# A two-layer graph attention kernel: h recomputed from x1 instead of stored, x1 written late, two steps of an epilogue moved to ACT

## What is computed

```python
h = relu(layernorm(x))
wh = h @ W;  e = wh @ a[:128] + (wh @ a[128:]).T
e = where(e > 0, e, 0.2 * e);  e = where(adj > 0, e, -9e15)
x1 = x + elu(softmax(e) @ wh)
h = relu(layernorm(x1))
Qn, Kn = cos_normalize(h @ Wq.T), cos_normalize(h @ Wk.T)
att = softmax(where(adj > 0, Kn @ Qn.T, -9e15))
out = x1 + 0.5 * (att @ h) + 0.5 * h
```

## Time and profile before

| | us |
|---|---|
| median of 3 runs | 2189.89 |
| lowest and highest | 2189.19, 2190.89 |
| profiled execution | 2189.39 |
| its span | 2187.6 |
| busy: PE, DVE, ACT, POOL | 2142.1, 1963.5, 1752.8, 33.0 |

### The profile page before, as it was taken

How to read it: one execution, slowest core, us unless ns; L and a number is a source line. 1 busy time by engine, 2 the same in 40 slices (tenths; PEclk the granted TensorE clock), 3 DMA queues, 4 the chain that set the end, 5 groups by cost and what they waited for, 6 DMA issues and landing times.

```text
span 2187.6 us, 63203 instructions
## 1 busy us (share of the span) xinstructions
PE 2142.1 (98%) x26185; PEld 1733.5 (79%) x26185; DVE 1963.5 (90%) x1686; ACT 1752.8 (80%) x1928; POOL 33.0 (2%) x43
## 2 busy tenths in 40 slices
PE   5999999999999979999999999999999999999998
PEld 5999999999999956777777777777777777777776
DVE  7999999999999858889888898898898898898987
ACT  6687778878788668888888888888888888888886
POOL 1000000000000030000000000000000000000000
PEclk9999999999999989999999999999999999999999
DMA  6899999999999916565565665665665666656653
GB/s 248 328 382 401 390 405 397 401 402 399 403 400 388 361 40 217 193 223 204 207 215 196 224 212 196 220 220 193 214 221 200 212 204 216 215 194 218 218 193 115
DMA packets 153732, 573.52 MB, mean 262 GB/s; under 512 B 9936, under 2 KB 10576, under 8 KB 153168
## 3 DMA queue, kind: packets, MB, share of 16 engines
q1 hardware_dynamic: 142176, 546.02, 68.3%
q10 hardware_dynamic: 11376, 24.91, 3.0%
HBM read 558.24 MB, written 12.65 MB: 261 GB/s over the span
## 4 chain that ended last, share of the span: by engine, by line
PE 95%; DVE 2%; ACT 1%; issue 1%; DMA 0%; POOL 0%; ACTq 0%; POOLq 0%; DVEq 0%
PE bank L1197 32%; PE bank L1245 30%; PE bank L1266 21%; PE bank L1261 10%; DVE hl_buf L726 1%; PE bank L1152 1%; PE bank L1172 0%; DVE hl_buf L714 0%; DMA ring<-adj 0%; ACT hl_buf L558 0%; ACT ring L619 0%; POOL hl_buf L401 0%; PE bank L1094 0%; PE bank L1134 0%; DMA q_buf<-x 0%
## 5 line engine op out<-in xcount | busy, mean ns | idle before, releaser
L619 ACT ACTIVATE ring<-bank,th_col 128x512 f32<-128x512 f32 x1024 | 647.1, 683 | 231.0 <-PE bank L1245 223.3
L988 DVE SCALAR_TENSOR_TENSOR ring<-ring 128x2048 f32<-128x2048 int32 x256 | 586.4, 2291 | 154.5 <-ACT ring L619 154.5
L1197 PE MATMUL bank<-v_buf,ring 128*128 128x129 f16 (+1 forms) x12288 | 711.9, 220 | 6.3 <-DVE ring L902 6.1
L1197 PEld LDWEIGHTS bank<-v_buf,ring 128*128 128x128 f16 x12288 | 707.8, 98 | 9.8 <-issue 8.9
L1245 PE MATMUL bank<-v_buf,q_buf 128*128 128x512 f16 x3072 | 706.4, 380 | 5.2 <-ACT ring L619 5.2
L1266 PE MATMUL bank<-u_buf,hl_buf 128*128 (+1 forms) x8192 | 704.3, 220 | 0.0
L1266 PEld LDWEIGHTS bank<-u_buf,hl_buf 128*128 128x128 f16 x8192 | 631.8, 98 | 55.9
L902 DVE SCALAR_TENSOR_TENSOR ring<-r_ring,th_word,ring 128x1024 f32<-128x1024 f32 x512 | 619.3, 1277 | 19.3 <-ACT ring L448 19.1
L993 DVE TENSOR_TENSOR hl_buf<-ring,hl_buf 128x2048 f16<-128x2048 f32 x256 | 584.5, 2284 | 0.0
L1261 PE MATMUL bank<-u_buf,hl_buf 128*128 (+1 forms) x2048 | 557.9, 272 | 0.5 <-DVE hl_buf L993 0.5
L448 ACT ACTIVATE ring<-ring 128x2048 f32<-128x2048 int32 x256 | 481.2, 1908 | 88.4 <-DMA ring<-adj 85.0
(11 more groups left out here) (138 smaller groups left out, 433.0 us busy)
## 6 DMA issues: line engine op xcount, KB each, us to landing
ring<-adj SPq DMA_DIRECT2D x512, 1024.0 KB, 5.6
r_ring<-a_rows SPq DMA_DIRECT2D x8, 512.0 KB, 7.0
x_dram<-q_buf ACTq DMA_DIRECT2D x8, 512.0 KB, 7.2
h_dram<-hl_buf ACTq DMA_DIRECT2D x8, 512.0 KB, 7.4
r_ring<-x_dram ACTq DMA_DIRECT2D x16, 256.0 KB, 4.2
r_ring<-h_dram ACTq DMA_DIRECT2D x16, 256.0 KB, 4.4
out<-r_ring ACTq DMA_DIRECT2D x16, 256.0 KB, 4.8
r_ring<-k_rows ACTq DMA_DIRECT2D x15, 256.0 KB, 4.1
```

Source lines behind the costliest of these rows:

```text
L619: ins = nc.scalar.activation(p_ring[:, k, (2 * hf + m) * IW:(2 * hf + m + 1) * IW], bank[:, 2 * hf + m, :], ACT.Exp, scale=q_scale[:, j:j ...
L988: V.scalar_tensor_tensor(p_ring[:, k, :], adj_ring[:, k, :], 0.0, p_ring[:, k, :], ALU.is_gt, ALU.mult).then_inc(s_m, 1)
L1197: ins = mm(acc0(par, it), weights0(k, ps)[:, it // 4, jj, f], v2[:, bass.ds((2 * j + us) * VW, D + 1)], start=False, stop=False, skip_grou ...
```

## The change

- DRAM no longer holds h. For the last sum of layer 1, `residual_h` computes it again from the loaded x1 with four Relus of 128 x 128 on ACT, at step (3, 2) of each chunk (in the first one at (2, 2)); for that, scale and bias of all 64 tiles are kept, each chunk's in its own columns.
- x1 of chunks 0, 4 and 7 is written as before, from ACT. That of 1, 5, 2, 6 and 3 is written from SP directly after the last load of adj for layer 0. Each copy of transposed h waits for the two writes whose memory it overwrites, on one of four semaphores.
- DVE's min(z, 0) goes. ACT computes relu(-z) and then exp(-that) in its place, one behind the other.
- DVE's cast of h to float16 goes. ACT copies h there behind its Relus, where it issued the write of h; DVE waits for that copy and subtracts.

Cut to its core (semaphores' declarations and the renaming of columns in `scale_bias` are left out):

```diff
+X1_EARLY = (0, 4, 7)
+X1_LATE = (1, 5, 2, 6, 3)
...
             chunks0(chunk)
+            for c in X1_LATE:
+                sp.wait_ge(s_ev, len(EPI0) * c + EPI0.index("x1") + 1)
+                sp.dma_start(x1_dram[:, c * C0:(c + 1) * C0], xs[:, c * C0:(c + 1) * C0]).then_inc(s_x1w[c % (NC0 // 2)], 16)
...
                 def exponential():
-                    act.wait_ge(s_ev, at("neg"))
-                    nc.scalar.activation(e_buf, e_buf, ACT.Exp).then_inc(s_ea, 1)
+                    act.wait_ge(s_free, c + 1)
+                    nc.scalar.activation(e_buf, z_buf, ACT.Relu, scale=-1.0).then_inc(s_neg, 1)
+                    act.wait_ge(s_neg, c + 1)
+                    nc.scalar.activation(e_buf, e_buf, ACT.Exp, scale=-1.0).then_inc(s_ea, 1)
 
                 def root():
-                    act.wait_ge(s_ev, at("x1"))
-                    act.dma_start(x1_dram[:, bass.ds(c * C0, C0)], xs[:, bass.ds(c * C0, C0)]).then_inc(s_x1w, 16)
+                    if c in X1_EARLY:
+                        act.wait_ge(s_ev, at("x1"))
+                        act.dma_start(x1_dram[:, bass.ds(c * C0, C0)], xs[:, bass.ds(c * C0, C0)]).then_inc(
+                            s_x1w[c % (NC0 // 2)], 16)
...
                     if lo == 0:
                         act.wait_ge(s_ev, at("nbias"))
-                        if not (isinstance(c, int) and c == 0):
-                            act.wait_ge(s_hw, 16 * c)
...
                     ins.then_inc(s_ea, 1)
                     act.wait_ge(s_ea, 3 * c + 3)
-                    act.dma_start(h_dram[:, bass.ds(c * C0, C0)], h_buf).then_inc(s_hw, 16)
+                    nc.scalar.activation(u_buf[:, bass.ds(c * IT0, IT0), 0:D], h_buf.rearrange("p (t f) -> p t f", f=D),
+                                         ACT.Copy).then_inc(s_uh, 1)
...
-            act.wait_ge(s_x1w, 16 * (NC0 - 1))
-
             def copy_ht(g):
+                act.wait_ge(s_x1w[g // 4], 32)
                 act.wait_ge(s_ht, g + 1)
...
-            act.wait_ge(s_x1w, 16 * NC0)
             copy_ht(12)
...
-            act.wait_ge(s_hw, 16 * NC0)
...
             def residual(i):
                 act.dma_start(e_x1, x1_dram[:, bass.ds(i * IW, IW)]).then_inc(s_fin, 16)
-                act.dma_start(e_h, h_dram[:, bass.ds(i * IW, IW)]).then_inc(s_fin, 16)
+
+            def residual_h(i):
+                act.wait_ge(s_fin, 16 * (i + 1))
+                for it in range(IT1):
+                    f, t = slice(it * P, (it + 1) * P), i * IT1 + it
+                    ins = nc.scalar.activation(e_h[:, f], e_x1[:, f], ACT.Relu, bias=nbias[:, t:t + 1], scale=rstd[:, t:t + 1])
+                ins.then_inc(s_eh, 1)
...
-                def negative():
-                    dve.wait_ge(s_free, c + 1)
-                    V.tensor_scalar(e_buf, z_buf, 0.0, None, ALU.min).then_inc(s_ev, 1)
...
-                    V.tensor_copy(hi, h8).then_inc(s_ev, 1)
-                    dve.wait_ge(s_ev, at("hi"))
+                    dve.wait_ge(s_uh, c + 1)
                     V.tensor_tensor(u_buf[:, bass.ds(c * IT0, IT0), D + 2:UW], h8, hi, ALU.subtract).then_inc(s_ev, 1)
...
-            dve.wait_ge(s_x1w, 16 * (NC0 - 1))
-
             def copy_ht(g):
+                dve.wait_ge(s_x1w[g // 4], 32)
...
-            dve.wait_ge(s_x1w, 16 * NC0)
             copy_ht(13)
...
-                    dve.wait_ge(s_fin, 32 * (i + 1))
+                    dve.wait_ge(s_eh, i + 1)
```

More of the change, by code:

```diff
@@ L59 @@
 EARLY = 4
+X1_EARLY = (0, 4, 7)
+X1_LATE = (1, 5, 2, 6, 3)
 FOLDS = (0, 16, 48, T)
 LN = ("diff", "total", "m2", "dsq", "between", "var", "rstd", "nbias")
-EPI0 = ("den", "neg", "elu", "x1", "stats") + LN + ("hi", "lo")
+EPI0 = ("den", "elu", "x1", "stats") + LN + ("lo",)
 EPI1 = ("some", "max", "recip", "scale", "keep", "kept", "lows", "y")
@@ L77, in graph_layers @@
         x1_dram = nc.dram_tensor("x1_dram", [P, N], F32, kind="Internal").ap()
-        h_dram = nc.dram_tensor("h_dram", [P, N], F32, kind="Internal").ap()
         k_rows = nc.dram_tensor("k_rows", [T, P], F32, kind="Internal").ap()
@@ L185, in graph_layers @@
         s_ev = sem("epilogue0_vector")
+        s_neg = sem("negative_part_ready")
+        s_uh = sem("h_high_ready")
         s_ea = sem("epilogue0_scalar")
-        s_x1w = sem("x1_written")
-        s_hw = sem("h_written")
+        s_x1w = [sem(f"x1_written{p}") for p in range(NC0 // 2)]
+        s_eh = sem("residual_h_ready")
         s_wkq = sem("wkq_in")
@@ L515, in normalised @@
                         ins = nc.scalar.activation(h_buf[:, it * P:(it + 1) * P], xs[:, bass.ds(c * C0 + it * P, P)],
-                                                   ACT.Relu, bias=nbias[:, it:it + 1], scale=rstd[:, it:it + 1])
+                                                   ACT.Relu, bias=nbias[:, c * IT0 + it:c * IT0 + it + 1],
+                                                   scale=rstd[:, c * IT0 + it:c * IT0 + it + 1])
                     if hi < IT0:
@@ L653, in chunk1 @@
                     quotient, store = epilogue1(i - 1, 1 - par)
-                    parts = {(0, 2): lambda: key_high(i + 1), (1, 1): quotient, (2, 1): store, (2, 2): lambda: residual(i),
+                    parts = {(0, 2): lambda: key_high(i + 1), (1, 1): quotient, (2, 1): store, (2, 2): lambda: residual(i), (3, 2): lambda: residual_h(i),
                              (2, 3): lambda: load_factors(i + 2)}
@@ L660, in chunk1 @@
                 else:
-                    parts = {(0, 0): lambda: load_factors(1), (1, 2): lambda: key_high(1), (2, 1): lambda: load_factors(2)}
+                    parts = {(0, 0): lambda: load_factors(1), (1, 2): lambda: key_high(1), (2, 1): lambda: load_factors(2),
+                             (2, 2): lambda: residual_h(0)}
                 for g in range(G1):
@@ L699, in variance, with scale_bias @@
                 V.scalar_tensor_tensor(var, sq, 1.0 / D, var, ALU.mult, ALU.add).then_inc(done, 1)
-            def scale_bias(lo, hi, at, done):
-                V.reciprocal(rstd[:, lo:hi], small[:, 4, lo:hi]).then_inc(done, 1)
+            def scale_bias(lo, hi, at, done, base=0):
+                to = slice(base + lo, base + hi)
+                V.reciprocal(rstd[:, to], small[:, 4, lo:hi]).then_inc(done, 1)
                 dve.wait_ge(done, at("rstd"))
-                V.scalar_tensor_tensor(nbias[:, lo:hi], small[:, 1, lo:hi], -0.5, rstd[:, lo:hi],
+                V.scalar_tensor_tensor(nbias[:, to], small[:, 1, lo:hi], -0.5, rstd[:, to],
                                        ALU.mult, ALU.mult).then_inc(done, 1)
@@ L843, in scales @@
                     dve.wait_ge(s_ea, 3 * c + 2)
-                    scale_bias(0, IT0, at, s_ev)
+                    scale_bias(0, IT0, at, s_ev, c * IT0)
                 def split():
@@ L849, in split @@
                     hi = u_buf[:, bass.ds(c * IT0, IT0), 0:D]
-                    V.tensor_copy(hi, h8).then_inc(s_ev, 1)
-                    dve.wait_ge(s_ev, at("hi"))
+                    dve.wait_ge(s_uh, c + 1)
                     V.tensor_tensor(u_buf[:, bass.ds(c * IT0, IT0), D + 2:UW], h8, hi, ALU.subtract).then_inc(s_ev, 1)
-                return denominators, negative, residual, moments, scales, split
+                return denominators, residual, moments, scales, split
             def split_weights():
@@ L889, in chunk @@
                 else:
-                    parts = dict(zip((3, 7, 10, 11, 15, 19), epilogue(c - 1, 1 - par)))
+                    parts = dict(zip((3, 10, 11, 15, 19), epilogue(c - 1, 1 - par)))
                     if c == 1:
@@ L946, in key_low @@
                                 ALU.subtract).then_inc(s_lo, 1)
-            denominators, negative, residual, moments, scales, split = epilogue(NC0 - 1, 1)
+            denominators, residual, moments, scales, split = epilogue(NC0 - 1, 1)
             copy_ht(1)
@@ L958, in _ @@
             copy_rows(0)
-            negative()
             copy_ht(7)
```

## The result

| us | before | after |
|---|---|---|
| median of 20 runs each | 2190.67 | 2194.72 |
| lowest and highest | 2189.19, 2194.53 | 2192.73, 2199.20 |
| ratio of the times, with its 95% interval | | 1.0019 (1.0013 to 1.0026) |
| profiled execution | 2189.39 | 2196.39 |
| its span | 2187.6 | 2194.5 |

So the change costs 4.05 us, between 2.8 and 5.7. The median lies just under the 0.2% (4.4 us) named ahead, though the interval reaches beyond it; the time is inside the forecast range, 0.3 us under its top, and the cost is four times the +1.05 of the forecast sum. The traces tell where, the medians how much.

The account below looks back on a forecast made before the run. PE was taken to bound the kernel, except between the layers. Terms -0.4 + 0 + 0 + 1.1 + 0.55 - 0.2 + 0 = +1.05 us took 2189.89 to 2190.9; range 2188.2 to 2195, chance 0.80.

Parts of the forecast that it names:

- Traffic in layer 0: Layer 0: removing seven h and five x1 writes gives 0 us, as PE's unit takes the same with idle DMA.
- The rival by which DMA set the pace: Layer 0: DMA bandwidth bounds PE after all, so dropping twelve writes saves 15.8 us, giving 2174; chance 0.05.
- The -0.4 for the last load: End of layer 0: less traffic and a lighter DVE shorten PE's waits for the first copies of transposed h; -0.4 us.
- Late writes: End of layer 0: five x1 writes behind the last load on its own queue cost 0 us, bounds 0 and 2.5.
- the late writes hold the last load: Rival, before PE's first q and k product: the load ends with all writes, 6.6 us more, 2197.5; chance 0.10.
- The Relu in chunks 1 to 6: Layer 0, forecast for chunks 1 to 7: ACT's Relu hides beside PE, 0 us, bounds -0.3 and +0.5.
- The Relu between the layers: Last epilogue: the Exp waits for the Relu on ACT's path, +1.1 us (0.95 to 1.3).
- The cast: Between the layers: ACT's Copy of h delays the key's high part, +0.55 us, bounds 0.5 and 0.75.
- Layer 1's start: Before layer 1's first exp: one DMA issue of h less, -0.2 us, bounds -0.35 and 0.
- Layer 1: Layer 1 chunks: four recomputing Relus, a 1.6 us burst on ACT, fit within 2.5 us of slack; 0 us.
- the table rival: Layer 1: ACT changes tables for Relu beside Exp; PE waits 0.75 us per chunk, 12 us, 2203; chance 0.03.
- The clock: Between the layers, PE's longer idle stretch behind the Exp: one low-clock stretch more or less, 2 us either way; chance 0.02.

Follow-up runs that it names:

- a5: The changed kernel with the late x1 writes waiting for the last load's landing and min(z, 0) back on DVE; median 2190.75 us, ratio to before 1.0002.
- a7: The changed kernel with late writes after the last load's landing, and both the minimum and the cast of h back on DVE; 2191.17 us, ratio 1.0002.
- a1: The changed kernel with SP waiting for the last adjacency load to land before it issues the five late x1 writes; 2193.15 us, ratio 1.0010.
- a10: a7 with the Relus that recompute h at step (3, 0) of each chunk instead of (3, 2); 2190.28 us, ratio to before 0.9994.
- a2: The changed kernel with all eight x1 writes issued by ACT in their epilogues, none late; 2192.43 us, ratio to before 1.0009.
- b2: The kernel before with only the negative part moved: Relu and Exp on ACT, no minimum on DVE; 2193.66 us, ratio 1.0012.
- a3: The changed kernel with min(z, 0) back on DVE and one Exp on ACT; 2193.12 us, ratio to before 1.0008.
- b1: The kernel before with only the five late x1 writes on SP directly behind the last load; 2193.74 us, ratio 1.0012.
- a9: The changed kernel with the five late x1 writes issued from ACT's queue instead of SP's; 2197.72 us, ratio to before 1.0028.
- a11: The changed kernel with all five late writes moved behind layer 1's first load, without a landing wait; 2195.14 us, ratio to before 1.0015.
- a4: The changed kernel with only the cast of h back on DVE; 2193.77 us, ratio to before 1.0015.

## Why the prediction was right, and where it was short

The time came out inside the range and under 0.2%, but not by the forecast sum; two of its zeros were wrong. The range held in part by luck. Its top had 2.5 for the last load, and that is what came; but the low clock behind PE's longer wait, 0.4 of the loss in layer 0 and the last step of layer 1 were in no bound, and 0.3 us were left. (Its bottom, 2188.2, leaves out the 0.7 of scatter named beside it: 2189.89 + 0.2 - 2 - 0.7 is 2187.4.)

- **Traffic in layer 0, 0 us: right.** A unit of chunk 7 still took 2.75 us and the long stretches of PE 57.4 ns per matmul (292.29 us for 5088). The rival by which DMA set the pace fell with it. The -0.4 for the last load can't be seen beside the scatter of that load: with the writes held back, PE's wait ahead of qk(0) was 0.00 us in a5 and a7, 0.18 in a1 and 1.28 in a10, for 0.38 in before.
- **Late writes, 0 us: wrong, 2.3 by the medians (bounds 0 and 2.5).** The step that failed was "I take **0**, as the writes use that same queue". The nearer row was the other one: 2.5 for a neighbouring write; the bound held, the choice within it didn't. The row taken for 0 had a load, and not a write, behind the load. The load grew by 2.3 us on average and by 3.2 in the profiled execution, so the rival "the late writes hold the last load" came in part, at 8.9 us, just short of the 9.0 from which it was to decide. Its price was too high, as the load lands ahead of the last writes (the five took 7.8 to 12.2 us, and were issued up to 3 us behind it). What neither had is the clock behind the longer wait. The Trainium skill ("DMA: Bandwidth & Descriptors", Queues, rings and completion order) has ring order; I had read from it that a later write on one ring takes nothing from an earlier load. The measurement decides against that reading. The same page (Two DMAs through the same engine are not ordered) says that descriptors of one queue start in order but are pipelined, and by this sentence a slower load is no surprise.
- **The Relu in chunks 1 to 6, 0 us (bounds -0.3 and +0.5): wrong, about +0.9.** The arithmetic "waits about 1.1 - 0.69 = 0.4 us" was done for chunk 2 alone, and "Other chunks have more" lead stood without rows. In chunk 3 DVE was out of masks for 2.53 us. The forecast counted the Relu's 1.06 on ACT but not that it makes the burst mask, Relu, table load, Exp 5.1 us long while masks wait, nor that the loads' landings scatter (4.9 to 8.9 us in after) and a late one takes from the same lead.
- **The Relu between the layers, +1.1: right**, 1.08 on ACT and 1.09 in PE's wait ahead of qk(6), the same in all kernels.
- **The cast, +0.55: right at its place** (+0.6 for the key's high part; PE's wait ahead of qk(12) grew by 0.43, from 6.38 us to 6.81, a little under the bound of 0.5), **but not seen in the time.** And the cast on DVE isn't free once the write of h is gone: with it there the low part of the key took a microsecond more, and the wait was 7.11.
- **Layer 1's start, -0.2: right.** The first exp of scores followed the warm exp by 0.11 us instead of 0.31 (821.77 to 821.88).
- **Layer 1, 0: right in the loop** (step, slack and tables as forecast; the table rival fell), **short by 0.34 at the end**, where the last chunk's burst has no idle gap behind it; a10 takes it away.
- **The clock** was a rival "near nothing" for the stretch behind the Exp. It came, at another place: behind the wait ahead of qk(0), worth about 1.3 us in the profiled execution. At its own place, qk(6) and qk(7) took 4.2 us together in before and in after.

By these terms the sum would have been 1.05 + 2.3 + 0.9 + 0.34 = 4.6, for 4.05 measured.

What stays open: what one write alone costs in time (its 1.3 us on the load are from one trace); why in a2 four chunks were stretched and in b2 hardly one; and what makes the last load vary between 5.0 and 6.9 us when no write is behind it.

## What to carry to other kernels

A load on which everything waits is not protected by being issued first, on the same queue or another: if the traffic behind it has slack, let it wait for that load's landing; here that cost nothing that PE waited for. Where a helper engine's lead is the cover for a burst, read the lead at every place where the burst occurs, not at one, and look at the last iteration by itself, since it has nothing to hide behind. Work moved off an engine with cover onto one that is on the serial path elsewhere is paid at full length there.

## What the runs showed of the hardware that I had not expected

- Five writes of 512 KB behind a 1 MB load on the same queue: it took 8.2 us on average (four kernels), without them 5.9 (seven). Against the load ahead of it in the same trace, it took 1.2 to 2.1 us more with them and 0.2 to 0.3 less without; with one write 1.08 more, and with five on the other queue 2.51 more (one trace each). In a1, where the last load had landed before them and the next ones left 4.0 us behind the first of them, the 2.62 MB of writes had landed 8.7 us after their first issue.
- A wait of PE of 2.55 to 4.67 us ahead of qk(0) was followed by a stretch at 0.50 of the clock in after, a3, b1 and a9, and waits up to 1.7 us never were. One of 2.93 (a11) was not either.
- The same 128x512 subtraction on DVE took 0.68 us or 1.75, and two operations on 128x8 that take 0.17 elsewhere took 1.13 and 1.18 in before (786.43 and 787.59 us). The long ones began while POOL's half sums were under way (in a4 at 799.21, the sum from 798.81 to 800.41; in before from 786.25 to 788.75); the short one of after began at 803.51, ahead of the sum at 803.77. The other way round, a mask operation of DVE that began at 756.08 in before, inside a half sum, kept its 1.27 us, and the sum took 2.53 instead of 1.27. The Trainium skill ("GPSIMD Engine Reference", Specifications) has GpSimd's SBUF interfaces shared with VectorE, with contention for DVE instructions in a 2-port mode or with two SBUF inputs. The subtraction has two such inputs and fits; the operation at 786.43 reads one, and which mode it ran in the traces don't show. No run here isolates it.
